# Two graph layers over one adjacency matrix: which rows a partition of a VectorE block takes, and where the accumulator's columns are put in order

## What is computed

```python
coefs = exp(-evals * t)[:, None]
h = x + adj @ (coefs * (adj.T @ x))   # einsum 'nk,nc->kc', then 'nk,kc->nc'
x = layernorm(h)
adj_hat = adj + eye(N); deg = sum(adj_hat, axis=1)
y = x + tanh(adj_hat / deg @ (x @ W) + b)
x = layernorm(y)
```

## Time and profile before

| | us |
|---|---|
| median of 3 runs | 702.49 (699.87 to 707.55) |
| the profiled execution | 704.87 |
| its span, first to last instruction | 703.1 |
| TensorE busy in the span | 636.9 (91%) |
| VectorE busy | 516.4 (73%) |
| ScalarE busy | 407.2 (58%) |
| GpSimd busy | 341.6 (49%) |

### The profile page before, as it was taken

One profiled execution on the slowest core, in us unless ns is written; L12 is line 12 of the kernel. 1 busy time (PEld: TensorE's weight loads), 2 busy tenths in 40 slices (PEclk: granted clock), 3 DMA queues, 4 the chain that ended last, 5 costly groups with the idle time before them and its releaser, 6 DMA issues.

```text
span 703.1 us, 9318 instructions
## 1 busy us (share of the span) xinstructions
PE 636.9 (91%) x3016; PEld 518.7 (74%) x3016; DVE 516.4 (73%) x648; ACT 407.2 (58%) x825; POOL 341.6 (49%) x167
## 2 busy tenths in 40 slices
PE   3899999999958779899998999999999799898983
PEld 3688888887747558677786888888888587777862
DVE  3699899998949787868774356465528589698975
ACT  4899999999944555535453435346325364554540
POOL 0000000002916677664929848767927738373751
PEclk9999999999988999999998999999999899999997
DMA  8999999999999999897969759788749789999900
GB/s 290 387 386 386 387 387 387 387 387 387 332 248 248 231 270 220 237 190 216 252 155 274 172 128 241 179 180 241 184 115 267 152 224 262 240 264 266 255 16 30
DMA packets 198582, 176.82 MB, mean 251 GB/s; under 512 B 6280, under 2 KB 147848, under 8 KB 198544
## 3 DMA queue, kind: packets, MB, share of 16 engines
q1 hardware_dynamic: 124080, 137.90, 65.3%
q10 hardware_dynamic: 74464, 38.43, 24.8%
HBM read 174.21 MB, written 2.10 MB: 251 GB/s over the span
## 4 chain that ended last, share of the span: by engine, by line
PE 49%; POOL 13%; DVE 12%; ACT 10%; issue 7%; DMA 4%; ACTq 4%; SPq 0%; POOLq 0%; DVEq 0%
POOL lo L320 11%; PE ps L659 10%; PE ps L661 10%; PE ps L660 10%; ACT hi L358 7%; PE ps L652 5%; DMA raw<-in_adj_dram 4%; PE ps L630 4%; PE ps L632 4%; PE ps L631 4%; DVE vt L474 3%; DVE lo L482 3%; ACTq L261 3%; ACT hi L373 2%; POOL rstd L315 1%
## 5 line engine op out<-in xcount | busy, mean ns | idle before, releaser
L320 POOL TENSOR_TENSOR lo<-vt,hi 128x1024 fp32r<-128x1024 f32 x119 | 296.8, 2524 | 166.9 <-ACT hi L373 166.9
L474 DVE STREAM_TRANSPOSE vt<-raw 128x1024 f32<-128x1024 f32 x138 | 167.8, 1229 | 58.8 <-PE ps L661 57.6
L373 ACT ACTIVATE hi<-vt 128x1024 fp32r<-128x1024 f32 x138 | 142.2, 1057 | 71.5 <-DVE vt L474 50.6
L455 DVE TENSOR_TENSOR lo<-raw,hi 128x1024 fp32r<-128x1024 f32 x120 | 154.4, 1287 | 21.6 <-ACT hi L358 19.1
L358 ACT ACTIVATE hi<-raw 128x512 fp32r<-128x512 f32 x256 | 158.5, 622 | 14.4 <-DMA raw<-in_adj_dram 8.7
L373 ACT ACTIVATE hi<-ps 128x1024 fp32r<-128x1024 f32 x62 | 63.4, 1028 | 116.1 <-PE ps L652 114.1
L659 PE MATMUL ps<-hi,s_hi 128*128 128x512 f32 x256 | 108.7, 425 | 8.2 <-POOL lo L320 7.9
L482 DVE TENSOR_TENSOR lo<-ps,hi 128x1024 fp32r<-128x1024 f32 x62 | 75.0, 1211 | 54.2 <-ACT hi L373 54.1
L630 PE MATMUL ps<-hi,xg_hi 128*128 128x512 f32 x256 | 102.8, 402 | 9.5 <-DVE lo L455 8.7
L659 PE MATMUL ps<-hi,p_hi 128*128 128x512 f32 x256 | 105.4, 412 | 4.2 <-POOL lo L320 3.1
L308 POOL TENSOR_TENSOR lo<-raw,hi 128x1024 fp32r<-128x1024 f32 x8 | 25.4, 3197 | 169.4 <-ACT hi L358 169.3
(11 more groups left out here) (60 smaller groups left out, 611.3 us busy)
## 6 DMA issues: line engine op xcount, KB each, us to landing
raw<-in_adj_dram SPq DMA_DIRECT2D x95, 1024.0 KB, 14.2
raw<-in_adj_dram SPq DMA_DIRECT2D x138, 256.0 KB, 5.6
raw<-in_adj_dram ACTq DMA_DIRECT2D x138, 256.0 KB, 6.4
out_dram<-o_g ACTq DMA_DIRECT2D x8, 256.0 KB, 3.7
x_sb<-in_x_dram SPq DMA_DIRECT2D x1, 1792.0 KB, 14.7
x_sb<-in_x_dram SPq DMA_DIRECT2D x1, 256.0 KB, 3.3
w_sb<-in_L_gnn_W_dram ACTq DMA_DIRECT2D x1, 64.0 KB, 6.1
b_bc<-in_L_gnn_b_dram ACTq DMA_DIRECT2D x1, 64.0 KB, 8.0
```

The lines of the kernel that those rows point to most:

```text
L320: nc.gpsimd.tensor_tensor(lo[:, slot(p), :], vt[:, slot(p), :], hi[:, slot(p), :].bitcast(f32), ALU.subtract).then_inc(pool_lo_ready, 1)
L373: nc.scalar.activation(hi[:, slot(s), :], src, ACT.Copy).then_inc(hi_ready, 1)
L455: nc.vector.tensor_tensor(lo[:, q % RING1, :], raw[:, k, 2 * h:2 * h + 2, :].rearrange("p r n -> p (r n)"), hi[:, q % RING1, :].bitcast(f3 ...
L474: nc.vector.transpose(vt[:, slot(s), :].rearrange("p (m b i) -> p m b i", m=2, b=RB), raw[:, BLOCKS[n].buf].rearrange("p r w -> p (r w)") ...
```

## The change

A partition of a VectorE quarter now takes 16 neighbouring rows (row 16 n + b) in place of rows 32 apart (row 32 b + n). The transfer's source is then 512 rows one after the other. TensorE's blocks are loaded as in pass 1, 4 neighbouring rows to a partition. So that both kinds of block still agree on their columns, the transposes write every column of their output to a new place, and the accumulators' columns hold row 16 n + b at column 32 b + n. They are put in order by the two instructions that take them out of PSUM, and the one matmul that adds x1 W to `acc3` is cut in four, each of which writes with steps.

```diff
-    adj_v = adj.rearrange("(g r p) (k w) -> g k p r w", r=R, p=P, w=CW)
     adj_x = adj.rearrange("(g p r) (k w) -> g k p r w", r=R, p=P, w=CW)
-    adj_q = adj.rearrange("(g b n) (k q w) -> g k q n b w", b=RB, n=QP, q=QN, w=P)
+    adj_q = adj.rearrange("(g n b) (k q w) -> g k q n b w", b=RB, n=QP, q=QN, w=P)
...
+    def by_rows(a):
+        return a.rearrange("p (b n) -> p n b", b=RB)
...
-                    sp.dma_start(raw[:, BLOCKS[n].buf], adj_v[group(BLOCKS[n].visit), BLOCKS[n].col])\
+                    sp.dma_start(raw[:, BLOCKS[n].buf], adj_x[group(BLOCKS[n].visit), BLOCKS[n].col])\
...
-                    nc.scalar.activation(stage[:, 0, :], acc2(v), ACT.Copy).then_inc(acc_out, 1)
+                    nc.scalar.activation(stage[:, 0, :].rearrange("c (n b) -> c n b", b=RB), by_rows(acc2(v)), ACT.Copy)\
+                        .then_inc(acc_out, 1)
...
-                    nc.vector.tensor_tensor(stage[:, par, :], acc_row(row), save(v), ALU.add).then_inc(sum3, 1)
+                    nc.vector.tensor_tensor(stage[:, par, :].rearrange("c (n b) -> c n b", b=RB), by_rows(acc_row(row)),
+                                            by_rows(save(v)), ALU.add).then_inc(sum3, 1)
...
-                        last = nc.tensor.transpose(turn_slot(s)[:, jj, r * P:(r + 1) * P],
+                        last = nc.tensor.transpose(turn_slot(s)[:, jj].rearrange("p (l r n) -> p r n l", l=R, r=R)[:, r],
                                                    raw[:, BLOCKS[n].buf, r, m * P:(m + 1) * P], ident[:, :])
...
-                    x1T = stage[:, 1, :] if g in BY_TENSOR else \
-                        stage[:, 1, :].rearrange("c (m q i) -> c q m i", m=JB, q=QN)
-                    nc.tensor.matmul(acc3(v), w_sb[:, :], x1T, start=v == 0, stop=True).then_inc(xw_done, 1)
+                    for m in range(JB):
+                        if g in BY_TENSOR:
+                            x1T = stage[:, 1, :].rearrange("c (n a b) -> c a b n", a=JB, b=JB)[:, m]
+                            dst = acc3(v)[:, m * P:(m + 1) * P].rearrange("c (b n) -> c b n", b=JB)
+                        else:
+                            x1T = stage[:, 1, m * P:(m + 1) * P].rearrange("c (q h b) -> c b q h", q=QN, h=2)
+                            dst = acc3(v).rearrange("c (b q m h) -> c m b q h", b=RB, q=QN, m=JB)[:, m]
+                        last = nc.tensor.matmul(dst, w_sb[:, :], x1T, start=v == 0, stop=v == 0 or m == JB - 1)
+                    last.then_inc(xw_done, 1)
```

## The result

| | before | after |
|---|---|---|
| median of 4 runs | 703.19 us | 716.34 us (712.53 to 718.98) |
| span of the profiled execution | 703.1 us | 717.2 us |

The changed kernel is slower: the ratio is 1.0171, with a 95% interval of 1.0129 to 1.0213, some 12 us. That lies inside the stated range (691 to 725 us) and 13.6 us above the forecast of 702.7.

What follows compares the result with a forecast made beforehand. TensorE was taken to bound 310 to 550 us, slow transfers 190 to 236 us. Profiled 704.87 us, x1 W +0.2, transfers, transposes, copies 0, gave 705.1; the median 2.4 under: 702.7 us, range 691 to 725.

Steps and rivals of the forecast that it cites:

- the side given 0.28: Whole kernel: slower by over 1%, by A, C or D together; chance 0.28.
- no change: Whole kernel: transfers and TensorE within a few per cent of before, 702.7 us; chance 0.52.
- C: Transfers in pass 2: the 16 engines meet in the same part of memory; 12 us slower, 714 us; chance 0.10.
- D: Copies out of PSUM: stepped reads double their time; +8 us, 710 us; chance 0.05.
- A: TensorE from 236 us on: stepped PSUM writes slow matmuls; 54 us slower, 757 us (half-way cases 720); chance 0.13.
- The matmul with x1 W, "+0.2": TensorE, eight times: 2 passes of 512 columns (0.86 us) become 8 instructions of 128 (0.89 us); +0.2 us in all.
- "+6.9": Matmul with x1 W on TensorE: other end of its term, if stepped PSUM writes doubled it; +6.9 us.
- The transfers, "0": Loads of pass 2, quarters and TensorE's 31 blocks: the new order of rows changes nothing; 0, ends 15 gained, 20 lost.
- The transposes, "0": TensorE, 496 transposes in 62 steps: stepped PSUM writes cost nothing; 0, other end +0.88 us a step.
- The copies, "0": ScalarE's copy and VectorE's sum, 8 times each: reading with a step of 128 bytes costs nothing; 0, together to 8 us.
- The chain from 190 to 236 us: Chain of waits there: 37.5% ScalarE's queue and 12.2% issue, 22.9 of 46 us, said to go by transfer speed.
- the 12.2% "issue": Share of issue in the chain from 190 to 236 us, counted as going by the speed of the transfers.

Runs made afterwards that it cites:

- old 15: Kernel of loads alone, no arithmetic: a quarter with 15 of the 16 pieces of each partition, old order of rows; new 15 lands no later than it.
- new 15: Kernel of loads alone, no arithmetic: a quarter with 15 of the 16 pieces of each partition, new order of rows; issue 0.31 us.

## Why the prediction came out as it did

The measured time is in the range, on the side given 0.28. The likeliest case, no change, was wrong, and none of the four rivals is what happened, so that it fell into the range is in good part luck: the upper part of it was drawn for C, D and half of A. By the steps:

- **The matmul with x1 W, "+0.2".** The step that failed most, by 7 us. I took "8 instructions of 128 columns, which the products just ahead of it show at 0.89 us", and those read straight. I had looked at the stepped write alone, and "each of which writes with steps" in the text on the change isn't even so for groups 0 and 1; the diff steps the moving operand in both of its branches. Read steps double an fp32 matmul (1.74 us for 0.89), and undoing them gives some 7 us back. The upper end that I kept, "+6.9", was right in size by another cause.
- **The transfers, "0".** Right for the memory: both orders run at 290 GB/s, and old 15 and new 15 take the same. Wrong for the queue: joined rows lengthen each issue from 0.31 to 0.56 us, 276 times. With the form held equal the new order costs nothing that shows (0.9957 against 0.9947), so the new quarters' 0.8% goes with the form. I wrote that "only the order of the pieces in memory changes"; the form in which the program states them changed as well. The issues that I had looked at were medians in full queues (some 0.5 us), which hide it; the minima show it, here ScalarE's, before and then after (min/median/max ns):

```profile
L261 ACTq DMA_DIRECT2D raw<-in_adj_dram x138: 317/512/3550, 184.8 to 654.8; - x138
L264 ACTq DMA_DIRECT2D raw<-in_adj_dram x138: 567/648/2897, 184.1 to 666.5; - x138
```

  The 31 TensorE blocks, put at 0 too, are lengthened as well (539 for 368 ns at the least, on SyncE's queue); their part of the time was not measured apart. And the trace before held a sign of it, in the minima of pass 1's loads of neighbouring rows and of pass 2's with rows apart, though pass 1's queue was rarely empty:

```profile
L273 SPq DMA_DIRECT2D raw<-in_adj_dram x64: 612/2434/4627, 1.2 to 170.7; - x64
L288 SPq DMA_DIRECT2D raw<-in_adj_dram x31: 368/385/2534, 175.5 to 659.8; - x31
```

- **The transposes, "0".** Right: 0.79 us to the next matmul before and after. Rival A, stepped writes, is refuted, also for fp32 matmuls. The Trainium skill, "PSUM — Partial Sum Buffer", section Specifications, says that any non-contiguous pattern slows matmuls significantly. The runs here disagree for writes by fp32 matmuls (3.75 for 3.73 us) and transposes (1.91 for 1.91), whose columns come at half the rate of fp32r (0.86 ns for 0.44); with fp32r it wasn't tried.
- **The copies, "0".** Right for ScalarE from PSUM. VectorE's sum grew to 1.04 us, for its SBUF operand, within the bound of a doubling; straightening it brought no time. Rival D named the right kind of cost, stepped reads, but for these two copies and not for the matmul.
- **Rival C** forecast the right sign with a mechanism that the loads alone don't show: 290 GB/s in both orders. The 238 for 257 GB/s in one stretch, which looked like its proof, is not one, since in the kernel with the new quarters alone the same 10 us show 263. A rate over 10 us of one execution is no measure here.
- **The chain from 190 to 236 us** was read rightly, ScalarE held by its own issues, but only as a place where faster transfers could pay. It said something plainer: let another queue issue. That the 12.2% "issue" beside it goes by the transfers too was assumed and isn't shown.

## What to carry to other kernels

Before stepping an operand, ask on which side: in these runs a stepped float32 operand in SBUF cost every engine (TensorE's moving operand double, VectorE and ScalarE half as much again), and a stepped one in PSUM cost nothing or little. Compare the issue time of transfers, by its minimum, when an access pattern changes, even if bytes and pieces stay. And when the chain names a compute engine's queue, try to move the issues to a queue that has nothing else to do before working on the transfers.

## What the runs showed of the hardware that I had not expected

- A source of rows at one step, joined into one dimension, took 0.25 us more to issue on SyncE's queue (560 for 311 ns), and as much on ScalarE's in the kernel (567 for 317 ns at the least), the same for 256 rows as for 512.
- Small pieces from two full queues start each burst at some 215 to 270 GB/s, apart from a higher first slice or two, and reach a steady 290 after some 7 to 10 us; one queue alone gave some 215.
- One order of those tried was slower: partitions on neighbouring rows with a partition's own rows 256 apart (4 MB) ran at about 200 to 240 GB/s, in its one stretch. Partitions 8 rows apart with the same 256 between a partition's own rows ran at 290. The Trainium skill, "DMA: Bandwidth & Descriptors", section Latency and other measured facts, has 103 GB/s for rows at a pitch of 4 MB from one partition to the next and 164 at 2 MB, where a padded pitch gave 214. Here the 4 MB lie within a partition, and partitions 2 MB apart ran at 290 in the two stretches that had them, so these loads do not show that rule. The third stretch, in slices of 1 us from 60 us:

```profile
GB/s 290 289 291 290 194 7 20 83 161 109 172 121 122 226 235 208 193 227 226 203 239 263 241 202 180 192 204 209 206 228 259 220 195 225 234 234 226 245 231 214
```
